# An unrolled first stage: half-size products, powers added out of PSUM, and V's scale found inside the stage

## The reference, cut to what matters

```
dtA  = A * exp(log_dt)                       # A is complex, one row per channel h, 64 states n
Cc   = B * C * (exp(dtA) - 1) / A
h    = 2 * real( sum over n of  Cc[c,h,n] * exp(dtA[h,n] * l) )      # l = 0..1023: the 1024 features
h    = h + attention(layernorm(h))           # 32 heads of 32, causal, 128 tokens
h    = h + ffn(layernorm(h))                 # quantised gate, up and down, 2752 wide
```

## Time and profile before

| | us |
|---|---|
| median of three runs | 2041.17 |
| the profiled execution | 2039.54 |
| its span, from first to last instruction | 2037.7 |
| PE busy | 1884.0 (92%) |
| DVE busy | 1163.9 (57%) |
| ACT busy | 615.4 (30%) |
| POOL busy | 614.3 (30%) |

### The profile page before, as it was taken

One profiled execution on the slowest core, in us unless ns is written; L12 is line 12 of the kernel. 1 busy time (PEld: TensorE's weight loads), 2 busy tenths in 40 slices (PEclk: granted clock), 3 DMA queues, 4 the chain that ended last, 5 costly groups with the idle time before them and its releaser, 6 DMA issues.

```text
span 2037.7 us, 31325 instructions
## 1 busy us (share of the span) xinstructions
PE 1884.0 (92%) x13212; PEld 1023.7 (50%) x13212; DVE 1163.9 (57%) x1476; ACT 615.4 (30%) x871; POOL 614.3 (30%) x261
## 2 busy tenths in 40 slices
PE   0377699999999999999999999999999999999999
PEld 0367566656666665545554444444444444444444
DVE  8999568777787878756644544444444445111011
ACT  2055333433433444421113333333333333200000
POOL 2676023433434333533112222223223222101101
PEclk9998699999999999999999999999999999999999
DMA  2022211111021222144433223223223222543341
GB/s 92 11 62 62 56 42 56 33 46 34 19 82 58 79 56 79 63 162 148 162 104 115 87 69 104 81 75 104 78 78 102 75 83 79 194 145 114 128 145 42
DMA packets 99812, 173.32 MB, mean 85 GB/s; under 512 B 13984, under 2 KB 75168, under 8 KB 91744
## 3 DMA queue, kind: packets, MB, share of 16 engines
q1 hardware_dynamic: 99680, 171.41, 26.2%
HBM read 114.22 MB, written 56.11 MB: 84 GB/s over the span
## 4 chain that ended last, share of the span: by engine, by line
PE 76%; DVE 7%; POOL 2%; issue 1%; ACT 1%; DMA 0%; ACTq 0%; DVEq 0%
PE acc L1140 15%; PE acc L1214 15%; PE acc L1141 15%; PE ps_p L944 3%; PE ps_p L946 3%; PE ps_p L945 3%; PE acc L1058 3%; PE acc L1060 2%; PE acc L1059 2%; PE ps_t L971 2%; PE ps_p L960 2%; PE ps_p L962 2%; PE ps_p L961 2%; PE ps_l L1156 2%; POOL prob L904 1%
## 5 line engine op out<-in xcount | busy, mean ns | idle before, releaser
L1140 PE MATMUL acc<-x_hi,q_f 128*128 128x512 f16 x1376 | 522.0, 379 | 0.0
L1141 PE MATMUL acc<-x_lo,q_f 128*128 128x512 f16 x1376 | 521.5, 379 | 0.0
L1214 PE MATMUL acc<-down_levels,hid_parts 128*128 128x512 f16 x1376 | 300.1, 379 | 0.0
L904 POOL TENSOR_TENSOR prob<-prob,mx 128x1024 f32<-128x1024 f32 x64 | 121.4, 1898 | 383.7 <-DVE mx L1497 383.7
L1140 PEld LDWEIGHTS acc<-x_hi,q_f 128*128 128x128 f16 x1376 | 134.6, 98 | 174.8 <-issue 17.8
L1214 PEld LDWEIGHTS acc<-down_levels,hid_parts 128*128 128x128 f16 x1376 | 133.2, 98 | 163.1 <-issue 5.0
L1141 PEld LDWEIGHTS acc<-x_lo,q_f 128*128 128x128 f16 x1376 | 134.7, 98 | 156.9
L915 POOL TENSOR_SCALAR q_f<-q_raw 128x2048 f16<-128x2048 int32 x22 | 118.0, 5366 | 314.1 <-PE acc L1141 312.5
L944 PE MATMUL ps_p<-x_hi,w_qk 128*128 128x512 f16 x512 | 194.7, 380 | 0.0
L945 PE MATMUL ps_p<-x_lo,w_qk 128*128 128x512 f16 x512 | 194.0, 379 | 0.0
L946 PE MATMUL ps_p<-x_hi,w_qk 128*128 128x512 f16 x512 | 194.0, 379 | 0.0
(11 more groups left out here) (285 smaller groups left out, 3072.5 us busy)
## 6 DMA issues: line engine op xcount, KB each, us to landing
q_raw<-in_gu_q SPq DMA_DIRECT2D x22, 1024.0 KB, 7.3
hidden_parts<-hidden SPq DMA_DIRECT2D x42, 512.0 KB, 3.5
hid_parts<-hidden_parts SPq DMA_DIRECT2D x15, 1376.0 KB, 6.5
down_raw<-in_down_q SPq DMA_DIRECT2D x22, 512.0 KB, 5.2
w_raw<-in_w_qk SPq DMA_DIRECT2D x8, 1024.0 KB, 4.9
h_tokens<-n_tok SPq DMA_DIRECT2D x16, 512.0 KB, 3.8
o_parts<-ot SPq DMA_DIRECT2D x32, 256.0 KB, 2.3
wv_raw<-in_w_o SPq DMA_DIRECT2D x8, 1024.0 KB, 5.1
```

The costliest lines, as they stand in the source:

```text
L904: nc.gpsimd.tensor_tensor(prob[s % 2][p][:], prob[s % 2][p][:], bc(mx[p][:], H, 2), ALU.subtract).then_inc(s_sub[p], 1)
L1140: nc.tensor.matmul(acc[u % 2][:, m, :], lev, x2_hi[:, k, tok], start=(k == 0), stop=False)
L1141: last = nc.tensor.matmul(acc[u % 2][:, m, :], lev, x2_lo[:, k, tok], start=False, stop=(k == KT - 1))
L1214: last = nc.tensor.matmul(acc[n % 2][:, b, :], parts[n % 3][:, at], levels[:, i, b * CH:(b + 1) * CH], start=(i == 0 and part == 0), stop= ...
```

## The change

The stage keeps its mathematics, but for one thing: the magnitudes are now 32 Exp operations on ACT, each with its step as the scale, instead of a product on POOL and one Exp.

- There is no hardware loop and there are no lags in registers: each engine's queue is written out for all steps, and the semaphores count up from zero.
- The preparation works in two halves of 64 channels (`heads(k)`) for the phases, the sines, the tables and the rotations. POOL has no part in it. The first half's tables and rotations come before the first unit, the second half's tables stand behind W(1), and its rotations behind W(2), W(3) and W(4).
- `ssm_ps` is two tensors of one bank, one for each half of a product, with its own evacuation. The two banks that this frees hold `v_second`: S writes to PSUM, and W reads one operand from PSUM.
- In step k, DVE does F(k+1), I(k-2), S(k+1), W(k+1), L(k-3), M(k-1). ACT does high(k-3), normalise(k-2), columns(k, first half), tokens(k-1), columns(k, second half), deviation(k-1). PE does the first half of product(k), tokens(k-1), the second half, features(k-2).
- `find_tops` comes before the first unit, `find_big` in DVE's step 6, SP's exchange behind the store of unit 7, `find_scale` in DVE's step 11. ACT's two pieces `high` and DVE's two pieces `low` of Wv come in step 15.
- `find_big` uses one operation less.

The core of the diff, in the order of the file (pieces for PSUM, SP, PE, ACT and DVE):

```diff
-        ps = [st.enter_context(nc.psum_tensor(f"ssm_ps{s}", [P, UH, P], F32)) for s in two]
+        ps = [st.enter_context(nc.psum_tensor(f"ssm_ps{s}", [P, UH // 2, P], F32)) for s in two]
+        v_second = st.enter_context(nc.psum_tensor("v_second", [P, UH * P], F32))
...
-            with sp.Fori(0, VIS) as n:
-                for s in two:
-                    sp.wait_ge(s_tok[s], n + 2)
-                    sp.dma_start(h0_dram[:, channels(n, s), :], tok[s][:]).then_inc(s_out[s], 16)
-            first.exchange(sp, 0)
+            for u in range(UNITS):
+                sp.wait_ge(s_tok, u + 1)
+                sp.dma_start(h0_dram[:, channels(u), :], tok[u % 2][:]).then_inc(s_out[u % 2], 16)
+                if u == UNITS - 9:
+                    first.exchange(sp, 0)
...
+            for k in range(UNITS + 2):
+                if each(0, k):
+                    product(k, 0)
+                if each(1, k):
+                    to_tokens(k - 1)
+                if each(0, k):
+                    product(k, 1)
+                if each(2, k):
+                    to_features(k - 2)
...
-            nc.scalar.activation(mag[:], mag[:], ACT.Exp).then_inc(s_mag, 1)
+            for k, step in enumerate(STEPS_OF):
+                last = nc.scalar.activation(mag[:, :, k], t[2][:], ACT.Exp, scale=float(step))
+            last.then_inc(s_mag, 1)
...
+            for k in range(UNITS + 3):
+                if each(3, k):
+                    high(k - 3)
+                if each(2, k):
+                    normalise(k - 2)
+                if each(0, k):
+                    columns(k, 0)
+                if each(1, k):
+                    tokens(k - 1)
+                if each(0, k):
+                    columns(k, 1)
+                if each(1, k):
+                    deviation(k - 1)
+                if k == UNITS - 1:
+                    act.wait_ge(s_v, UNITS)
+                    for part in two:
+                        first.high(nc, act, 0, part)
...
+            dve.wait_ge(s_mag, 1)
+            tables(0)
+            dve.wait_ge(s_tab, 1)
+            for part in range(3):
+                rotations(0, part)
+            first.find_tops(nc, dve, chain)
...
+            for k in range(-1, UNITS + 3):
+                if each(-1, k):
+                    second_factor(k + 1)
+                if each(2, k):
+                    inverse(k - 2)
+                if each(-1, k):
+                    second_power(k + 1)
+                    power(k + 1)
+                if each(3, k):
+                    low(k - 3)
+                if k == 0:
+                    tables(1)
+                    dve.wait_ge(s_tab, 2)
+                if 1 <= k < 4:
+                    rotations(1, k - 1)
+                if k == UNITS - 10:
+                    first.find_big(nc, dve, chain, 0)
+                if k == UNITS - 5:
+                    first.find_scale(nc, dve, chain, 0)
+                if each(1, k):
+                    mean(k - 1)
+                if k == UNITS - 1:
+                    for part in two:
+                        first.low(nc, dve, 0, part)
```

More of the change, by code:

```diff
@@ L147, in four, with channels, heads, each @@
             return room.rearrange("p (h a b) -> p h a b", h=UH, b=n)
[L149 to L172, removed]
+        def channels(u, start=0, end=UH):
+            return slice(u * UH + start, u * UH + end)
+        def heads(k):
+            return slice(k * HALF_H, (k + 1) * HALF_H)
+        def each(lag, k):
+            return 0 <= k - lag < UNITS
         @block.sync
@@ L258, in _ @@
             quarter = half[5]
-            nc.scalar.activation(tab1[:, :, 0:2 * TI], tab1[:, :, 0:2 * TI], ACT.Sin, scale=-TWO_PI, bias=quarter[:]).then_inc(s_trig, 1)
-            nc.scalar.activation(tab1[:, :, j0], tab1[:, :, j0], ACT.Sin, scale=half[1][:], bias=half[3][:]).then_inc(s_trig, 1)
-            nc.scalar.activation(tab2[:, :, i], phase[:, :, i], ACT.Sin, scale=TWO_PI).then_inc(s_trig, 1)
-            nc.scalar.activation(tab2[:, :, j1], phase[:, :, j1], ACT.Sin, scale=half[1][:]).then_inc(s_trig, 1)
@@ L285, in high @@
-            def high(n, s):
-                apart(act, s_passed, (s_trn[s], n + 2))
-                nc.scalar.activation(xn_hi[:].rearrange("p k (c h) -> p k c h", h=H)[:, :, :, channels(n, s)],
-                                     pn[:].rearrange("p k (c h) -> p k c h", h=UH), ACT.Copy).then_inc(s_hi[s], 1)
-            run(act, [(2, columns), (4, deviation), (3, tokens), (4, normalise), (5, high)])
-            first.high(nc, act, 0, 0)
-            first.high(nc, act, 0, 1)
+            for k in two:
+                hs = heads(k)
+                act.wait_ge(s_phase, k + 1)
+                nc.scalar.activation(tab1[:, hs, 0:2 * TI], tab1[:, hs, 0:2 * TI], ACT.Sin, scale=-TWO_PI, bias=quarter[:])
+                nc.scalar.activation(tab1[:, hs, j0], tab1[:, hs, j0], ACT.Sin, scale=half[1][:], bias=half[3][:])
+                nc.scalar.activation(tab2[:, hs, i], phase[:, hs, i], ACT.Sin, scale=TWO_PI)
+                nc.scalar.activation(tab2[:, hs, j1], phase[:, hs, j1], ACT.Sin, scale=half[1][:])
+                nc.scalar.activation(tab2[:, hs, j0], tab2[:, hs, j0], ACT.Sin, scale=half[2][:], bias=half[4][:]).then_inc(s_trig, 1)
```

284 lines of the change are left out of this document (146 added, 138 removed).

## The result

| | before | after |
|---|---|---|
| median, us | 2040.62 (2038.68 to 2045.85, 4 runs) | 2010.92 (2010.42 to 2012.98, 4 runs) |
| the profiled execution | 2039.54 | 2011.06 |
| its span | 2037.7 | 2009.3 |

What follows compares the result with a forecast made beforehand. DVE, partly waiting for POOL's running operations, was taken to bound the first stage; 109.5 + 80 + 26.7 = 216.2 against 236.7, 20.5 less, gave 2021 us. Likeliest case 2014 to 2029, range cut at 2009 and 2033.

Steps and rivals of the forecast that it cites:

- no wait of PE for ACT in the steady part: Rival in the units: PE's features wait for ACT's late normalise, making the kernel slower, 2052 at pitch 11; chance 0.05.
- S at 1.1 beside a running POOL operation: Sign of being wrong, in the units: S, writing PSUM, would run at 1.1 us without waiting for POOL.
- more than forecast: First-stage rival: clock holds, S waits for nobody, faster tail, 2011; DVE alone setting the pitch, 2004; under 2014, chance 0.16.
- Front: Start to the end of W(5): predicted 109.5 us, against 117.04 before.
- Ten units: W(5) to W(15): pitch 7.9, ten units 79, find_big 0.3 and find_scale 0.7, sum 80 us.
- clock loss: PE's products in the units slowed by a lower granted clock: 0.4 us per unit, on a pitch of 7.5.
- Tail: W(15) to the second stage's first product: predicted 26.7 us, 10.3 less than the 37.0 before.
- in waits for unit 15: Tail: V's two pieces high (1.15 each) and low (1.24 each) stand in step 15, in waits for unit 15.
- W leaves the alternation … that change pays little here: Units: W reading PSUM no longer takes turns with POOL, but POOL idled beside W anyway, so little gain.
- S keeps its lock: Units: S, with two SBUF inputs, still waits for POOL though it writes PSUM; otherwise 212.6 instead of 216.2.
- The loops: Units: writing out the hardware loops was taken at 0, with bounds of 0 and 2 us.
- The exchange: Units: SP's exchange behind unit 7's store was costed at nothing, up to 3 us if stores come late.

Runs made afterwards that it cites:

- second profile: The changed kernel run once more, unaltered, in a later group, and profiled again: 2013.04 us.
- b_unrolled: The kernel before with its hardware loops written out by Python on all five queues, nothing else: 2036.53 us.
- Experiment 2: Changed kernel with all tables and rotations before the first unit: 2012.82 us; that kernel with S writing to SBUF again: 2024.25 us.
- Experiments 1: Changed kernel with M(k-1) put before L(k-3) in DVE's steps: 2026.65 us; the same exchange alone in the kernel before: 2041.21 us.
- b_low_first: The kernel before with L(k-5) put before M(k-3) in DVE's steps, loops and sum in SBUF kept: 2041.21 us.
- experiment 3: Changed kernel with the magnitudes' exponents by one POOL product and one Exp again: 2019.67 us.
- experiment 4: V's scale found late and V's parts last in the changed kernel: 2018.93 us; scale found early in the kernel before: 2041.96 us.

## Why the prediction was right or wrong

**Right** was the direction, and the mechanism at nearly each place: the start of the coefficients' chain near 33 (32.5), L363's 0.3 (0.29), a and b at 46.8 (46.3), F ending 0.7 behind POOL, L at 1.2 behind W, columns in halves of 0.59, no wait of PE for ACT in the steady part, a second stage of unchanged length. S at 1.22 beside POOL's w1 was listed as a sign of being wrong ("S at 1.1 beside a running POOL operation"); it is none, since w1 waits for S there. The measured time, 2010.9, lies in the range; the case "more than forecast" is the one that came, through a sum of small terms, not through the mechanism it named for its far end.

**The sum, term by term.** Predicted 216.2 and measured 208.5:
- *Front*, 1.9 too much (3.9 by the second profile). One of it is the start: the load of the parameters is issued at 3.96, not 4.97, so the semaphore increments that I took at 0 seem to be worth their upper bound of 1.0. `b_unrolled` keeps them and issues the load at 4.82; no run takes them out alone. In between, the forecast for W(5) is right in part by luck: W(3) was put at 93.5 and ends at 88.4, and W(4) then takes 11.7 us where 6.4 were forecast, two errors of 5 us that cancel.
- *Ten units*, 80 predicted, 77.0 and 80.9 measured. A unit without clock loss was given 7.5; POOL starts at +7.0 and not +7.45, since the product's two halves and the tokens between them overlap more than the sum of their durations, and by the same formula (7.0 + 7.5, halved) the pitch is 7.25. With 1.0 for the scale and all of PE's extra time below this adds up to 76.9 and 81.6. That is a sum and not a proof: the formula has one pitch and an F that always waits for w0, while the trace has units of 6.6 to 8.9 us, v at +7.0 behind only some of the W, and an F that waits for v in one unit and for w0 in the next. The forecast also let only half of the clock's loss through. The rest, then, is put to the clock: in the first profile two of the half products lasted longer than 1.95 (3.13 and 3.49) and the features ahead of them too (1.56 and 1.19 instead of 1.05), 3.4 us in all; in the second four products (3.62, 3.62, 2.47, 3.53) and three features (1.94 each), 8.1 us. The granted clock over the units is 0.96 and 0.87. The loss to the clock is there, and its size differs from one execution to the next; the 4 us of the forecast lie between.
- *Tail*, 26.7 predicted and 24.0 measured, twice. The product of unit 15 ended at 6.8 and not 8.8: I had charged half of it at the low clock, and it had the full one. The meeting with POOL (1.8) didn't happen; 1.3 passes between the last L and the second stage. The text put V's parts "in waits for unit 15", while its own sum has normalise(14) behind V low; the trace bears out the sum (I(14) straight behind V low), so the 3 us were in the forecast without being named as a cost.

From the stage to the median: the profiled execution ended 8.0 us below its forecast (2019.0), the 7.7 of the stage and 0.3, and the median of the runs stood 1.6 above the profiled execution before and 0.1 below it after.

**"W leaves the alternation … that change pays little here" was wrong.** Experiment 2 gives 11.4 us. The prediction argued with the phase of the kernel before, in which POOL idles beside W in most units. But the same change moves that phase: with L ahead of M the product ends 1 us earlier, and v starts earlier against the next W. In the forecast's own numbers, v starts 0.05 us before the following W's end at a pitch of 7.5. In the trace, v starts inside W or ahead of it in six of the nine units 6 to 14, in three of them straight behind w1. So the sum assumed the free W that PSUM gives, while its words put no price on it. Experiments 1 and 2 fit together: L first gains nothing with W in SBUF (`b_low_first`), and taking it back costs 14 to 16 us with W in PSUM and the short lags. No run has W in SBUF with M ahead of L in the new kernel, so the shares of the two are not separated.

**S keeps its lock.** S(0) lasts 2.94 with its output in PSUM, 1.1 past the end of POOL's v(1) at 61.90, and S costs the same in both rooms in experiment 2. The Trainium skill, page "SBUF — State Buffer", section "SBUF: two separate sides", lets a DVE operation with two SBUF inputs contend for the lock, and the trace agrees. The same section counts a DVE operation in a 2-port mode among those that need it. In which mode an operation ran no trace shows; one-input operations that waited are the 128x128 multiplication that lasts 7.08 us beside POOL's 7.08 in experiment 3, and L574's 1.78 here.

**The loops** were taken at 0 with bounds of 0 and 2; alone, in the kernel before, they are worth 4.3 us. I had counted DVE's idle time only, and assumed that DVE's waits would swallow it.

**Halving the preparation** was taken as part of what brings W(5) forward. By itself it shows no gain (experiment 2); what counts more is that POOL leaves the preparation, 6.6 us for the magnitudes alone. POOL's product for tab2 has no run of its own; L363's 8.90 beside it became 0.29.

**The exchange** cost nothing where it lies now, as forecast, and DVE waits 10.6 us for it where it lies late.

## What to carry to other kernels

Where two engines share a lock, price an operation's move by the phase that the whole change leaves, not by the phase of the trace before: reordering one queue shifts when the other engine starts, and a step that met nobody may meet it in every second round. Where the lock bounds the loop, take such a step out of it (here by one operand in PSUM) together with the reordering. And before believing a shorter stage in one trace, take a second profile and the spread of the times: here two traces of one kernel differ by 3.9 us in ten units, and the slow products and features in them by 4.7. Work that stands "in waits" is only free if nothing queued behind it was ready: V's parts held up a normalise that was.

## What the runs showed of the hardware that was not expected

- An operation of 128x1 elements with two SBUF tensors lasts 0.16 us alone and 1.70 beside POOL's w0; one of 128x16 with one tensor 0.17 (experiment 4, POOL idle) and 1.78. Here a small size didn't keep an operation out of the wait.
- A hardware loop of five turns on five engines cost 4.3 us in the kernel before, where DVE idled only 3.5 us in ten units.
- Two executions of one kernel had granted clocks of 0.96 and 0.87 over the same ten units, with the same instructions. All six slow half products stand right behind features for which PE had waited between 2.41 and 3.74 us; other waits as long (2.95 ahead of 117.51) were followed by full speed.
